# Two attention and FFN layers on one core: values in one stretch per unit, ten probability steps, zero rows by ScalarE, biases added by GpSimd, and another order on SP

## What is computed

```python
xn = layernorm(x)
x = x + L0_attn(xn) + L0_ffn(xn)   # 32 heads of 16, 8 kv heads, softmax(q k / 4) v, Wo
                                   # ffn: gelu(xn W1 + fc1_bias) W2 + fc2_bias, 2048 wide
xn = layernorm(x)
x = x + L1_attn(xn) + L1_ffn(xn)   # qkv with bias, rope, causal mask, softmax(q k / 16) v, dense + b_dense
                                   # ffn: (silu(x1) * x2) w3 + b3, 512 wide
```

## Time and profile before

| | us |
|---|---|
| median of 3 runs | 619.87 |
| the runs | 623.91, 619.87, 619.39 |
| the profiled execution | 624.43 |
| its span | 622.3 |
| mean granted TensorE clock in it | 0.981 of 2.4 GHz |

### The profile page before, as it was taken

How to read it: one execution, slowest core, us unless ns; L and a number is a source line. 1 busy time by engine, 2 the same in 40 slices (tenths; PEclk the granted TensorE clock), 3 DMA queues, 4 the chain that set the end, 5 groups by cost and what they waited for, 6 DMA issues and landing times.

```text
span 622.3 us, 10485 instructions
## 1 busy us (share of the span) xinstructions
PE 577.9 (93%) x3232; PEld 443.3 (71%) x3232; DVE 451.5 (73%) x1198; ACT 356.0 (57%) x611; POOL 217.8 (35%) x332
## 2 busy tenths in 40 slices
PE   2698899999999999999999998899989989899997
PEld 2686677787777878667777777677767877666754
DVE  6559967656566675576897677889997988578663
ACT  3337766755555683676694575657655654465541
POOL 5712423122303321211223122354644555254241
PEclk9999899999999999999999999989999999988989
DMA  5583542353223244315443332425433344334101
GB/s 186 176 241 127 141 115 67 105 153 103 68 86 103 70 131 124 86 45 160 120 136 101 95 90 74 120 85 139 141 98 102 86 127 130 87 102 116 23 5 63
DMA packets 29806, 67.29 MB, mean 108 GB/s; under 512 B 4788, under 2 KB 17588, under 8 KB 27704
## 3 DMA queue, kind: packets, MB, share of 16 engines
q1 hardware_dynamic: 21112, 38.32, 22.2%
q0 software_dynamic: 8640, 28.32, 15.6%
HBM read 51.67 MB, written 14.68 MB: 107 GB/s over the span
## 4 chain that ended last, share of the span: by engine, by line
PE 73%; DVE 9%; ACT 6%; issue 5%; DMA 5%; POOL 1%; SPq 1%; ACTq 0%; DVEq 0%; POOLq 0%
PE banks L692 49%; PE banks L745 8%; PE banks L771 7%; PE banks L793 7%; DMA q_sb<-q_parts 2%; DVE banks L1065 1%; DMA q_sb<-max_t 1%; ACT L910 1%; PE banks L774 1%; PE banks L712 1%; ACT hid_f L930 1%; ACT L929 1%; DVE bn L976 1%; ACT probs L910 1%; DVE x_res L1109 1%
## 5 line engine op out<-in xcount | busy, mean ns | idle before, releaser
L910 ACT ACTIVATE probs<-banks 128x512 f32<-128x512 f32 (+1 forms) x256 | 137.6, 545 | 185.1 <-PE banks L771 143.9
L692 PE MATMUL banks<-xnT,w_up 128*128 128x512 f32 x576 | 154.7, 403 | 5.4 <-issue 3.8
L1070 DVE TENSOR_REDUCE neg_max<-banks 128x2 f32<-128x512 f32 x128 | 87.1, 687 | 93.2 <-PE banks L745 92.6
L692 PE MATMUL banks<-w_down,hid 128*128 128x512 f32 x480 | 131.1, 407 | 4.5 <-ACT hid_f L930 2.0
L692 PEld LDWEIGHTS banks<-xnT,w_up 128*128 128x128 f32 x576 | 103.4, 192 | 33.9 <-issue 15.1
L1065 DVE CUSTOM_DVE_ANT_0 banks<-banks,mask_qk 128x128 f32<-128x128 f32 (+1 forms) x256 | 86.3, 374 | 39.4 <-PE banks L745 39.4
L692 PEld LDWEIGHTS banks<-w_down,hid 128*128 128x128 f32 x480 | 87.7, 193 | 32.3 <-DVE neg_max L1070 6.7
L745 PEld LDWEIGHTS banks<-k_sb,q_sb 96*128 96x128 f32 x512 | 93.7, 193 | 23.3 <-issue 5.2
L745 PE MATMUL banks<-k_sb,q_sb 96*128 96x256 f32 (+1 forms) x512 | 100.8, 279 | 5.2 <-DMA q_sb<-q_parts 4.0
L648 POOL TENSOR_SCALAR_AFFINE_SELECT probs<-probs 128x256 f32<-128x256 f32 x128 | 59.6, 466 | 102.6 <-ACT probs L910 97.5
L771 PE MATMUL banks<-q_sb,k_sb 97*128 97x512 f32 x192 | 79.9, 416 | 8.8 <-ACT probs L910 6.9
(11 more groups left out here) (77 smaller groups left out, 651.3 us busy)
## 6 DMA issues: line engine op xcount, KB each, us to landing
q_sb<-q_parts SPq DMA_DIRECT2D x64, 256.0 KB, 4.4
raw<-in_up POOLq DMA_DIRECT2D x48, 256.0 KB, 3.0
raw<-in_down POOLq DMA_DIRECT2D x40, 256.0 KB, 3.1
q_parts<-stage SPq DMA_DIRECT2D x32, 256.0 KB, 2.5
raw<-in_attn POOLq DMA_DIRECT2D x20, 256.0 KB, 3.2
k_parts<-stage SPq DMA_DIRECT2D x16, 256.0 KB, 2.6
k_sb<-k_parts SPq DMA_DIRECT2D x16, 256.0 KB, 4.0
x_res<-in_x SPq DMA_DIRECT2D x4, 512.0 KB, 4.0
```

The source lines that it names most:

```text
L692: mm = nc.tensor.matmul(out_ap, lhs(a), rhs(b_), start=first and j == 0, stop=stop and j == 2, **kw)
L910: nc.scalar.activation(probs[:, i, 0:w], banks[:, ST_BANKS[k % 2], 0:w], ACT.Exp, scale=SCALES[n // B]).then_inc(exp_done, 1)
L1070: nc.vector.tensor_reduce(neg_max[:, s, 2 * g:2 * g + 2, t], banks[:, bank_of[x], :].rearrange("p (r t) -> p r t", r=2)[:, :, 0:w], AX.X, ...
```

## The change

- Both pv steps of unit u-1 stand in slot 1 of unit u, next to each other; slot 5 has none. In the last unit both stand in `end_slots`.
- `probs` is a ring of ten places over all steps (`st_index(u, i) % 10`), and the exponential of step k waits for the pv that read step k-10.
- `neg_max` is two places of 128 columns, of which 16 are maxima and the rest zeros, and mt transposes all 128 columns. The triangular addend of layer 1's maxima is bfloat16.
- ScalarE writes the zero rows of the three q buffers ("fill"), from one column of zeros, two ahead of the first square root, one in a later slot of the start. GpSimd makes `k_sb`'s zero rows ahead of the wait for x, and its loads from the fifth piece on follow the low parts in the list.
- SP loads batch 0 of x in two DMAs with a semaphore each; in the start, the loads of k stand with those of q, a slot later, behind the store of q; "out" stands behind the next mrow.
- The biases come as three arrays already repeated over 128 partitions (256 KB each). GpSimd adds the two of layer 1 ("bias"), then adds a bias tile to each tile of x once its layernorm is done ("plus", 16 in all: six in unit 3, two in units 7, 11, 15, 19 and 23). The matmuls with ones, the split by VectorE and the memsets for them go.
- Layernormed x of later batches is transposed one slot later (slots 5 and 6).

```diff
-    o = [[("stats", 0, 0), ("root", 0, 0), ("rstd", 0, 0), ("ln", 0)] + split(0, "attn", 4, 5)]
+    o = [[("fill", 0), ("fill", 1), ("stats", 0, 0), ("root", 0, 0), ("rstd", 0, 0), ("ln", 0)] + split(0, "attn", 4, 5)]
...
-    o += [parts(("qkv", 0, 0)) + [("load_k", 0, 0), ("load_k", 0, 1)]]
-    o += [[("xn", 1, 0), ("xn", 1, 1), ("load_q", 0), ("load_q", 1)] + split(0, "up", 0, 1)]
+    o += [parts(("qkv", 0, 0))]
+    o += [[("xn", 1, 0), ("xn", 1, 1), ("fill", 2), ("load_k", 0, 0), ("load_k", 0, 1), ("load_q", 0), ("load_q", 1)] + split(0, "up", 0, 1)]
...
-        slots[1].append(("pv", u - 1, 1))
+        slots[1] += [("pv", u - 1, 0), ("pv", u - 1, 1)]
...
-    slots[5].append(("pv", u, 0))
...
+    if s == 3 and n + 2 < 2 * B:
+        for c in ((0, 1, 2) if n == 0 else (n + 2,)):
+            slots[2 if n else 2 * c].append(("plus", c // B, TT * (c % B)))
+            slots[4 if n else 2 * c + 1].append(("plus", c // B, TT * (c % B) + 1))
...
-        slots[4].append(("xn", n + 2, 0))
-        slots[5].append(("xn", n + 2, 1))
+        slots[5].append(("xn", n + 2, 0))
+        slots[6].append(("xn", n + 2, 1))
...
-    return [[("pv", u, 1), ("norm", u, 0), ("norm", u, 1), ("norm", u, 2), ("norm", u, 3), ("ctx", u)] + a[:3] + b[:3], a[3:] + b[3:]]
+    return [[("pv", u, 0), ("pv", u, 1), ("norm", u, 0), ("norm", u, 1), ("norm", u, 2), ("norm", u, 3), ("ctx", u)] + a[:3] + b[:3], a[3:] + b[3:]]
...
-        o.insert(k + 1, ("out", tile))
+        rows = [j for j, x in enumerate(o) if j > k and x[0] == "mrow"]
+        o.insert((rows[0] if rows else k) + 1, ("out", tile))
...
-        probs = sb("probs", [P, 8, 512])
-        neg_max = sb("neg_max", [P, S, UH, TT])
+        probs = sb("probs", [P, PROBS, 512])
+        neg_max = sb("neg_max", [P, 2, P])
...
-        bias_out = sb("bias_out", [P, 2, D], F32R)
-        ones = sb("ones", [P, P], F32R)
+        bias_out = sb("bias_out", [P, 2, D])
         ident = sb("ident", [P, P])
-        mask_qk = sb("mask_qk", [P, T])
+        zero = sb("zero", [P, 1])
+        mask_qk = sb("mask_qk", [P, T], BF16)
...
-        bias_raw = probs[:, 6:8, :]
+        bias_more = probs[:, PROBS - 1, :]
...
+            if x[0] == "plus":
+                eng.wait_ge(plus_done, pls[x] + 1)
+            else:
+                eng.wait_ge(wk_emptied, em[x if x[0] == "wo" else ("down",) + x[1:]] + 1)
 
...
-            load_x(0)
+            for t in range(TT):
+                sp_.dma_start(x_res[:, t, :], x_in[0][t * P:t * P + P, :]).then_inc(x_loaded[0] if t else x_first, 16)
...
                 if x[0] == "load_bias":
-                    sp_.wait_ge(made, ZEROED)
-                    for row in (0, 32):
-                        sp_.dma_start(bias_raw[row:row + 2, :, :], out_b).then_inc(bias_loaded, 16)
+                    for k, to in enumerate((bias_out[:, 0, :], bias_out[:, 1, :], bias_more)):
+                        sp_.dma_start(to, out_b[k]).then_inc(bias_loaded, 16)
...
+            nc.gpsimd.memset(zero[:, :], 0.0).then_inc(made, 1)
+            pool.wait_ge(made, 1)
             load(0)
             load(1)
             nc.gpsimd.memset(ident[:, :], 0.0).then_inc(made, 1)
-            pool.wait_ge(made, 1)
+            pool.wait_ge(made, 2)
             nc.gpsimd.affine_select(out=ident[:, :], in_=ident[:, :], compare_op=ALU.not_equal, fill=1.0,
                                     base=0, pattern=[[-1, P]], channel_multiplier=1).then_inc(made, 1)
             pool.wait_ge(made, IDENT)
+            nc.gpsimd.memset(k_sb[64:ROWS, :, :].bitcast(F32), 0.0).then_inc(made, 1)
+            pool.wait_ge(made, K_ZERO)
             pool.wait_ge(x_loaded[0], 16)
             load(2)
             load(3)
-            nc.gpsimd.memset(k_sb[64:ROWS, :, :].bitcast(F32), 0.0).then_inc(made, 1)
-            pool.wait_ge(made, 3)
-            load(4)
-            load(5)
-            nc.gpsimd.memset(k_sb[MROW:MROW + 1, :, :].bitcast(F32), 1.0).then_inc(made, 1)
-            pool.wait_ge(made, 4)
-            for k in range(RING):
-                load(6 + k)
-                nc.gpsimd.memset(q_sb[64:ROWS, k, :, :].bitcast(F32), 0.0).then_inc(made, 1)
-                pool.wait_ge(made, 5 + k)
             nc.gpsimd.memset(v_sb[:, :, :, :], 1.0).then_inc(made, 1)
             pool.wait_ge(made, ONES_V)
-            nc.gpsimd.memset(bias_raw[:, :, :], 0.0).then_inc(made, 1)
-            pool.wait_ge(made, ZEROED)
-            nc.gpsimd.memset(ones[:, :].bitcast(F32), 1.0).then_inc(made, 1)
-            pool.wait_ge(made, 10)
+            nc.gpsimd.memset(neg_max[:, :, :], 0.0).then_inc(made, 1)
+            pool.wait_ge(made, MAX_ZERO)
+            nc.gpsimd.memset(k_sb[MROW:MROW + 1, :, :].bitcast(F32), 1.0).then_inc(made, 1)
+            pool.wait_ge(made, ALL_MADE - 2)
             nc.gpsimd.memset(mask_qk[:, :], 0.0).then_inc(made, 1)
-            pool.wait_ge(made, 11)
+            pool.wait_ge(made, ALL_MADE - 1)
             nc.gpsimd.affine_select(out=mask_qk[:, P:], in_=mask_qk[:, P:], compare_op=ALU.is_ge, fill=MASKED,
                                     base=0, pattern=[[-1, P]], channel_multiplier=1).then_inc(made, 1)
...
-                    tri = probs[:, i, 0:512 if i < 4 else 2 * P].rearrange("p (r t) -> p r t", r=2)[:, :, 0:P]
+                    tri = probs[:, st_index(u, i) % PROBS, 0:512 if i < 4 else 2 * P].rearrange("p (r t) -> p r t", r=2)[:, :, 0:P]
...
+                if x[0] == "bias":
+                    pool.wait_ge(bias_loaded, 48)
+                    in_order()
+                    nc.gpsimd.tensor_tensor(bias_out[:, 1, :], bias_out[:, 1, :], bias_more, ALU.add).then_inc(bias_summed, 1)
+                    done[0] = (bias_summed, 1)
+                if x[0] == "plus":
+                    _, L, tile = x
+                    n, t = B * L + tile // TT, tile % TT
+                    pool.wait_ge(ln_done, TT * n + t + 1)
+                    if add_before[x]:
+                        wait_tile_sum(pool, add_before[x])
+                    in_order()
+                    nc.gpsimd.tensor_tensor(x_res[:, tile, :], x_res[:, tile, :], bias_out[:, L, :], ALU.add).then_inc(plus_done, 1)
+                    done[0] = (plus_done, pls[x] + 1)
...
-                    if x == ("m", 0, 0):
-                        pe.wait_ge(made, Q_ZERO)
+                    if u < RING and i == 0:
+                        pe.wait_ge(made, K_ZERO)
+                        pe.wait_ge(q_zeroed, u + 1)
...
-                    nc.tensor.transpose(banks[0:TT * UH, k, 0:P], neg_max[:, s, :, :].rearrange("p h t -> p (h t)"),
-                                        ident[:, :]).then_inc(wk_filled, 1)
+                    nc.tensor.transpose(banks[:, k, 0:P], neg_max[:, u % 2, :], ident[:, :]).then_inc(wk_filled, 1)
...
-                        p_ = probs[:, 4 * t + g, :]
+                        p_ = probs[:, st_index(u, 4 * t + g) % PROBS, :]
...
-                    if opens and rest == 0:
-                        pe.wait_ge(bias_split, 1)
-                        nc.tensor.matmul(banks[:, k, :], ones[:, :], bias_out[:, L, :],
-                                         start=True, stop=False, skip_group_check=True)
...
-                                   lambda h: w_down[:, c % 2, h, :], rest > 0 and e == 0, e == 1, skip_group_check=True)
+                                   lambda h: w_down[:, c % 2, h, :], e == 0, e == 1, skip_group_check=True)
...
+                if x[0] == "fill":
+                    act.wait_ge(made, 1)
+                    nc.scalar.copy(q_sb[64:ROWS, x[1], :, :].rearrange("p g t -> p (g t)"),
+                                   zero[64:ROWS, :].to_broadcast([ROWS - 64, UH * T])).then_inc(q_zeroed, 1)
...
-                    if k == 6:
-                        act.wait_ge(bias_split, 1)
-                    if u:
-                        act.wait_ge(pv_done, 2 * (u - 1) + t + 1)
+                    if k == PROBS - 1:
+                        act.wait_ge(bias_summed, 1)
+                    if k >= PROBS:
+                        act.wait_ge(pv_done, (k - PROBS) // 4 + 1)
                     w = 2 * P if n >= B and t == 1 else 512
-                    nc.scalar.activation(probs[:, i, 0:w], banks[:, ST_BANKS[k % 2], 0:w], ACT.Exp,
+                    nc.scalar.activation(probs[:, k % PROBS, 0:w], banks[:, ST_BANKS[k % 2], 0:w], ACT.Exp,
...
-                if x[0] == "bias":
-                    dve.wait_ge(bias_loaded, 32)
-                    link(nc.vector.tensor_copy(bias_out[:, :, :], bias_raw[:, :, :]))
-                    nc.vector.tensor_tensor(bias_out[32:64, :, :], bias_raw[32:64, :, :],
-                                            bias_out[32:64, :, :].bitcast(F32), ALU.subtract).then_inc(bias_split, 1)
...
-                    if n:
-                        dve.wait_ge(wk_filled, wk[("mt", u - S)] + 1)
+                    if u >= 2:
+                        dve.wait_ge(wk_filled, wk[("mt", u - 2)] + 1)
+                    if u == 0:
```

(7 more changed lines are left out.)

18 lines of the change are left out of this document (12 added, 6 removed).

## The result

The changed kernel takes 615.03 us (median of 4 runs, 609.33 to 616.99) against 621.62 (4 runs) for the kernel before on the same chip: a ratio of 0.9863 (95% interval 0.9824 to 0.9902). The forecast was 603 with a range of 593 to 614: the sign was right, the size was not, and the time lies outside the range. The profiled execution took 616.01, its span is 614.3. Run again on another chip, it took 615.26 (614.37 to 617.51), a ratio of 0.9887 (0.9854 to 0.9919), span 612.9. Times here are medians of all executions of a kernel on one chip; the ratios leave out the few that ran clearly slower or at a lower clock (in the table of experiments two of before_merge at 636 and 638, one of after_out_behind_sum at 2345.87, one of before_merge_xn_later at 909.93 and one of best_of, the profiled one, at 638.11).

A forecast was written before the change was run, and what follows sets the result against it. TensorE was taken to bound layer 0's units 1 to 15, and layer 1 only partly. Terms summed to -19.4 us, 605.0 from the profiled execution; from the median, 619.9 - 16.4 gave about 603, range 593 to 614.

The forecast's parts named there:

- Merge, -7.2: Both layers: one stretch of values per unit saves 0.30 us of TensorE each, 4.5 in layer 0, 2.7 in layer 1.
- No new wait: Moved value steps: neither ScalarE's exponential, waiting for its buffer, nor VectorE's norm behind slot 2's maximum would wait longer.
- the factor of 0.6: Layer 1: a microsecond taken from TensorE was counted as 0.6 us of the span.
- xn one slot later: 0: Transposes of layernormed x one slot later: no effect on time, since their users are a unit away.
- Biases, -2.0 and -1.2, and +1.5: 16 bias matmuls gone saves 2.0 us, VectorE's bias split gone 1.2; GpSimd's additions in layer 1 cost 1.5.
- Start, -2.5: Start-up: first q store 3.4 us earlier by VectorE and SP's order, less 0.9 for bias loads and a zero row.
- SP's order, -7.0 (4 for the median): Layer 1: stores behind the next maxima row remove TensorE's waits and slow clock, 7.0 us; 4 counted against the median.
- Tail, -1.0: End: last unit's first pv fits TensorE's 0.95 us wait for GpSimd's last mask, and slot 5 gains 1.0 us.
- Layer 1 keeps its time: Rival, chance 0.20: VectorE and GpSimd's masks bound layer 1, so gains there return as waits; about 611 us.
- The merge's rival: Rival, chance 0.08: the array empties between the two value steps too, the stretch keeps its overhead; 610 us.
- GpSimd's additions: Rival, chance 0.07: 16 additions on GpSimd's in-order queue, half on the path, cost 10 us instead of 1.5; 612.
- The likeliest case: The forecast's own sum of all terms, chance 0.60: about 603 us, 594 to 609 with its unknown terms.

The follow-up runs named there:

- before_merge: Kernel before with both value steps in slot 1 and the ring of ten, nothing else: 634.27 us, ratio 1.0130.
- after_out_behind_sum: Changed kernel with each store of a finished tile right behind its last addition again: 620.5 us, ratio 0.9969.
- before_merge_xn_later: Kernel before with the merged value steps and xn's transposes in slots 5 and 6: 627.08 us, ratio 1.0048.
- best_of: Changed kernel with merge and earlier maxima transpose in layer 0 only, q ahead of k's second half, bias loads later: 607.41 us, ratio 0.9740.
- after_xn_back: Changed kernel with xn's transposes back in slots 4 and 5: 623.94 us, ratio 1.0007.
- after_start: Changed kernel with the first root ahead of ScalarE's zero rows and GpSimd's last memset behind the first layernorm: 615.10 us, ratio 0.9846.

## Why the prediction was wrong

**Merge, -7.2.** The step that failed is "No new wait", written of both ScalarE's buffer and VectorE's norm. Those two were indeed without a new wait. I had asked who waits for the stretch in its new place, and not what its old place had covered. The size was right, 0.32 a unit against 0.30, and 5.1 in layer 0 against 4.5 once nothing stood in its way. What it had covered, in slot 5 of layer 0's units 2, 6, 10 and 14, was the 1.19 us from the last scores over VectorE's maximum to the next step that opens a bank: 0.86 to 0.95 us stand there in the changed kernel, and the earlier transpose takes them away. In the changed kernel layer 0 kept 2.8 of the merge's gain (second chip against its two-stretch version). In layer 1 the factor of 0.6 should have been zero or below: -2.7 expected, +2.6 measured (217.8 against 215.2), most of it in unit 27 and the clock behind it. VectorE has the same 177.6 us of work there as before (177.7), and what TensorE saves it waits.

**"xn one slot later: 0".** Wrong as an edit within this change: with the merge it is worth 7 to 9 us in the changed kernel and 5 in the kernel before, without it 0. My reason, that its users are a unit away, looks only at who needs the result; the step also needs a bank.

**Biases, -2.0 and -1.2, and +1.5.** Layer 0 and 1 stream 0.9 and 1.8 us less for the 12 matmuls (0.23 each), but in layer 1 no such gain is left in the stage's length; no run takes the bias matmuls out alone. Unit 0 lost 3.3 instead of 1.2, TensorE's streams are 2.1 us shorter there (the bias matmuls and a value step leave it, which I had put at 0, hidden under VectorE), and VectorE's rows 2.9 shorter (20.5 to 17.6), so that both gave way together. For the additions I charged 1.5 us in units 19 and 23; those units take as long with them as without, and the 1 to 3 us by the ratios are within the scatter.

**Start, -2.5.** Two steps failed. The store was to be issued 3.4 us earlier (1 by VectorE, 2.4 by SP's order) and was issued 1.83 earlier. And it was to bring its load, and the first matmul, earlier by as much. With the DMA engines at a share of 1.00 the path took 10.6 us from the store's issue to the first matmul (23.36 to 34.00) instead of 10.0 (25.19 to 35.22), and the maxima's phase then ran partly at the lower clock (0.81 from 34 to 48). The stage came out at +1.2 and, on the second chip, -0.4. The zero rows on ScalarE also stand in the way of the first root, which I had not seen; that cost nothing, as q's transfer hides it.

**SP's order, -7.0 (4 for the median).** Right: 5.2 undone, 5.0 alone, and 7.1 in layer 1 of the two traces, against 4 for the median and 7.0 for the profiled execution.

**Tail, -1.0.** Right: the stage kept its 7.3 with one value step more in it, and the last unit is 0.8 us shorter with the merge (9.5 against 10.3). The table counts that 0.8 to layer 1.

**The rivals.** "Layer 1 keeps its time" (0.20) had the mechanism for layer 1: with SP's order taken off, layer 1 gained nothing. It left layer 0 its gain, and so stood at 611. The first criterion I had set, layer 1 below 215, and the second, layer 0's middle 4 us shorter, were both missed. The merge's rival, an array that empties between its steps, was wrong: the stretch takes 1.86 us and not twice 0.99. GpSimd's additions were not on the path, and the clock did not fall: 0.98 in layer 1 against 0.96. The likeliest case summed seven gains as if each stayed, and its range, 594 to 609, left no room for a merge that gives next to nothing in either layer.

**Open.** Why the merge costs the kernel before 8 us by the ratio: its one trace, of the fastest run, shows 2.6 more in layer 0's middle and 0.8 less in layer 1. That its other executions have more stretches at the lower clock behind the same waits would fit the next section, but no trace of one was taken. In layer 1 the traces show where the merge's loss stands, in unit 27 above all, but no edit moved ScalarE's table loads there to show that they alone make it.

## What to carry to other kernels
A step that needs none of the scarce buffers is filler, and when it is moved, its old place has to be read as closely as the new one: list which neighbouring steps open a bank, and when the last bank comes free. A saving on the busiest engine is real only once the waits around it are no longer than before; test it with its cover restored, layer by layer. And when the transfer engines are full, a transfer issued earlier lands earlier by less: 1.2 us for 1.8 here, and nothing for 2.7. Taking bytes from ahead of it brought 2.2 us in one trace and next to nothing in two.

## What was not expected of the hardware
- A memset of a single partition (1x2048) on GpSimd, 1.80 us long, made VectorE's TENSOR_SCALAR of 128x2 elements beside it take 1.48 us; it takes 0.17 alone. Other operations it did not hold: a TENSOR_TENSOR of the same size, begun inside the same memset at 7.74, took 0.16 as it does alone, and in the kernel before two 128x512 subtractions begun inside such a memset (from 12.91 on) took 1.28 together.
- Like waits are not always followed by the lower clock. The pair of 1.06 and 1.20 us (0.97 and 1.15 in the fourth place) with one transpose between was followed by 3.4 us at the 1.2 GHz level in two of four places of after_xn_back and in none of four of before_merge; a pair of 0.95 and 1.44 in the changed kernel (271.6 to 274.9) was followed by one, and in its second trace not. In the traces used here a low stretch lasted 3.4 or 6.8 us, and once 10.2 (in the start of after_start); it costs about half its length.
- Sixteen value records in one row take 1.86 us, eight take 0.99: the second eight cost 0.87.
